# Conditioned residual product on one Trainium2 core: loads in 8 KB rows, zero blocks filled by ScalarE, placing shared with VectorE, first load in two parts

## What is computed

```python
w = weights[conditions]
return x + jnp.einsum('bct,bcd->bdt', x, w)
```

## Time and profile before

| | us |
|---|---|
| median of 3 runs | 48.3 |
| lowest, highest | 47.49, 48.56 |
| the profiled execution, its own time | 47.52 |
| its span in the profile | 45.6 |
| mean granted TensorE clock | 0.981 |

### The profile page before, as it was taken

One profiled execution on the slowest core, in us unless ns is written; L12 is line 12 of the kernel. 1 busy time (PEld: TensorE's weight loads), 2 busy tenths in 40 slices (PEclk: granted clock), 3 DMA queues, 4 the chain that ended last, 5 costly groups with the idle time before them and its releaser, 6 DMA issues.

```text
span 45.6 us, 301 instructions
## 1 busy us (share of the span) xinstructions
PE 23.4 (51%) x98; PEld 10.0 (22%) x98; DVE 14.9 (33%) x20; ACT 14.6 (32%) x18; POOL 2.6 (6%) x10
## 2 busy tenths in 40 slices
PE   0004000000000009999999789999999999930000
PEld 0004000000000004243527054534534434300000
DVE  0891000000003980009559290064064065550000
ACT  0820000000000009009999999062062063450000
POOL 4080900000000000000000000000000000000000
PEclk9999999999999999999999999999999999999975
DMA  0689999999999999999997999999998999999991
GB/s 0 108 338 431 424 417 431 417 439 424 431 431 511 431 403 417 388 460 460 460 331 280 403 424 453 381 489 446 460 417 338 431 446 403 424 439 388 417 406 47
DMA packets 2162, 17.83 MB, mean 391 GB/s; under 512 B 242, under 2 KB 242, under 8 KB 498
## 3 DMA queue, kind: packets, MB, share of 16 engines
q1 hardware_dynamic: 2016, 16.78, 89.1%
q0 software_dynamic: 144, 1.05, 5.4%
q10 hardware_dynamic: 2, 0.00, 0.0%
HBM read 9.44 MB, written 8.39 MB: 391 GB/s over the span
## 4 chain that ended last, share of the span: by engine, by line
PE 43%; DMA 21%; DVE 10%; ACT 7%; issue 5%; POOL 2%; POOLq 1%
PE product L156 31%; DMA gathered<-weights,table_row 21%; PE product L160 12%; DVE w_all L186 5%; ACT y_sb L116 4%; ACT w_diag L111 3%; POOL w_diag L128 2%; DVE w_diag L168 2%; DVE y_sb L195 2%; DVE gathered L183 1%; POOLq L36 1%; DVE piece L171 0%; DVE one L169 0%
## 5 line engine op out<-in xcount | busy, mean ns | idle before, releaser
L160 PE MATMUL product<-x_sb,w_all 64*64 64x512 f32 x64 | 8.9, 698 | 13.0 <-DVE w_all L186 12.9
L156 PE MATMUL product<-x_sb,w_diag 128*128 128x512 f32 x32 | 14.0, 594 | 0.3 <-issue 0.3
L191 DVE COPY y_sb<-product 128x1024 f32<-128x1024 f32 x7 | 8.6, 1225 | 12.6 <-PE product L156 7.2
L116 ACT COPY y_sb<-product 128x1024 f32<-128x1024 f32 x7 | 7.1, 1012 | 8.5 <-PE product L156 6.3
L111 ACT COPY w_diag<-w_all 64x256 f32<-64x256 f32 x8 | 5.1, 637 | 14.6 <-DVE w_all L186 14.4
L156 PEld LDWEIGHTS product<-x_sb,w_diag 128*128 128x128 f32 x32 | 6.0, 190 | 8.3 <-issue 8.3
L160 PEld LDWEIGHTS product<-x_sb,w_all 64*64 64x64 f32 x64 | 3.5, 207 | 17.6 <-DVE w_all L186 13.0
L183 DVE TENSOR_TENSOR gathered<-gathered,piece 128x64 f32<-128x64 f32 x1 | 0.3, 270 | 10.0 <-DMA gathered<-weights,table_row 10.0
L139 PE MATMUL product<-one,row_along 1*128 1x1 f32 x2 | 0.6, 344 | 3.6 <-DVE row_along L175 3.6
L186 DVE STREAM_TRANSPOSE w_all<-gathered 128x2048 f32<-128x2048 f32 x1 | 2.3, 2311 | 0.0
L195 DVE COPY y_sb<-product 128x512 f32<-128x512 f32 x2 | 1.4, 692 | 1.5 <-PE product L156 1.5
(11 more groups left out here) (4 smaller groups left out, 0.4 us busy)
## 6 DMA issues: line engine op xcount, KB each, us to landing
out<-y_sb SPq DMA_DIRECT2D x5, 1024.0 KB, 6.2
x_sb<-x SPq DMA_DIRECT2D x4, 1024.0 KB, 8.3
x_sb<-x SPq DMA_DIRECT2D x2, 2048.0 KB, 19.9
out<-y_sb SPq DMA_DIRECT2D x1, 2048.0 KB, 6.7
out<-y_sb SPq DMA_DIRECT2D x2, 512.0 KB, 4.3
condition<-conditions ACTq DMA_DIRECT2D x1, 0.2 KB
gathered<-weights,table_row POOLq DMA_INDIRECT x1, 9.7
```

The source lines that it names most:

```text
L116: nc.scalar.copy(y_sb[:, 4 * turn:4 * turn + 2, :], product[turn % SETS][0][:, :, :]).then_inc(moved_by_act, 1)
L156: product_of = nc.tensor.matmul(product[turn % SETS][j][:, g, :], w_diag[:, n - 4 * TILED, :], x_sb[:, n, :], start=True, stop=True)
L160: product_of = nc.tensor.matmul(product[turn % SETS][h][halves(g), j, :], w_all[halves(h), :, n], x_sb[halves(h), n, :], start=True, stop= ...
L191: nc.vector.tensor_copy(y_sb[:, 4 * turn + 2:4 * turn + 4, :], product[turn % SETS][1][:, :, :]).then_inc(moved_by_dve, 1)
```

## The change

Five edits are made together.

1. **8 KB rows.** `LOADS` and `STORES` are gone. Each turn is one load and one store of 1 MB (turn 7 is still stored in two halves), so nothing has 16 KB rows, and turn 2 is stored without waiting for turn 3.
2. **First load in two parts.** The load of turn 0 is issued as 16 partitions and then 112 partitions; TensorE waits for 32 on its semaphore. The other loads have semaphores of their own.
3. **Zeros by ScalarE.** The two memsets of `w_diag`'s off-diagonal blocks by VectorE and GpSimd are removed. VectorE sets a small tile `zero` (128x1), and ScalarE copies it, broadcast, to both blocks before it waits for `w_ready`.
4. **Shared placing.** ScalarE places only half 0 of each later turn, VectorE half 1, each ahead of its own move of the turn. TensorE waits for both.
5. VectorE's identity addition now waits for `pieces_set` itself, which GpSimd's removed memset no longer does.

```diff
-    LOADS = [(0, 0), (1, 1), (2, 2), (3, 3), (4, 5), (6, 7)]
-    STORES = [(0, 0), (1, 1), (2, 3), (4, 4), (5, 5), (6, 6)]
...
+        zero = sbuf("zero", [P, 1], fp32)
...
         def _(sp):
-            for first, last in LOADS:
-                pairs = pairs_of(first, last)
-                sp.dma_start(x_sb[:, pairs, :], x[:, pairs, :]).then_inc(x_loaded[first], 16)
-            for first, last in STORES:
-                sp.wait_ge(moved_by_act, last + 1)
-                sp.wait_ge(moved_by_dve, last + 1)
-                pairs = pairs_of(first, last)
-                sp.dma_start(out[:, pairs, :], y_sb[:, pairs, :]).then_inc(stored, 16)
+            for part in (slice(0, P // 8), slice(P // 8, P)):
+                sp.dma_start(x_sb[part, pairs_of(0), :], x[part, pairs_of(0), :]).then_inc(x_loaded[0], 16)
+            for turn in range(1, TURNS):
+                sp.dma_start(x_sb[:, pairs_of(turn), :], x[:, pairs_of(turn), :]).then_inc(x_loaded[turn], 16)
+            for turn in range(LAST):
+                sp.wait_ge(moved_by_act, turn + 1)
+                sp.wait_ge(moved_by_dve, turn + 1)
+                sp.dma_start(out[:, pairs_of(turn), :], y_sb[:, pairs_of(turn), :]).then_inc(stored, 16)
...
         def _(act):
             act.dma_start(condition[:, :, :], conditions).then_inc(condition_loaded, 16)
+            act.wait_ge(zero_set, 1)
+            for h in range(PAIR):
+                nc.scalar.copy(w_diag[halves(h), :, (1 - h) * D:(2 - h) * D],
+                               zero[halves(h), :].unsqueeze(2).to_broadcast([C, PAIRS - 4 * TILED, D])
+                               ).then_inc(w_zeroed, 1)
+            act.wait_ge(w_ready, 1)
             for turn in range(TURNS):
                 if turn < TILED:
-                    later = slice(4 * turn, 4 * turn + 4)
-                    act.wait_ge(w_ready, 1)
-                    for h in range(PAIR):
-                        nc.scalar.copy(w_diag[halves(h), later, h * D:(h + 1) * D],
-                                       w_all[halves(h), :, pairs_of(TILED + turn, TILED + turn)].rearrange("p d n -> p n d")
-                                       ).then_inc(w_placed, 1)
+                    nc.scalar.copy(w_diag[halves(0), pairs_of(turn), 0:D],
+                                   w_all[halves(0), :, pairs_of(TILED + turn)].rearrange("p d n -> p n d")
+                                   ).then_inc(w_placed_by_act, 1)
...
         def _(pool):
-            pool.wait_ge(pieces_set, 2 * (P // Q))
-            nc.gpsimd.memset(w_diag[halves(1), :, 0:D], 0.0).then_inc(w_zeroed, 1)
...
         def _(pe):
-                if turn in x_loaded:
-                    pe.wait_ge(x_loaded[turn], 16)
+                pe.wait_ge(x_loaded[turn], 32 if turn == 0 else 16)
...
                 if turn >= TILED:
-                    pe.wait_ge(w_placed, PAIR * (turn - TILED + 1))
+                    pe.wait_ge(w_placed_by_act, turn - TILED + 1)
+                    pe.wait_ge(w_placed_by_dve, turn - TILED + 1)
...
         def _(dve):
-            nc.vector.memset(w_diag[halves(0), :, D:PAIR * D], 0.0).then_inc(w_zeroed, 1)
+            nc.vector.memset(zero[:, :], 0.0).then_inc(zero_set, 1)
...
+            dve.wait_ge(pieces_set, 2 * (P // Q))
             dve.wait_ge(w_gathered, 16)
...
             for turn in range(LAST):
+                if turn < TILED:
+                    nc.vector.tensor_copy(w_diag[halves(1), pairs_of(turn), D:PAIR * D],
+                                          w_all[halves(1), :, pairs_of(TILED + turn)].rearrange("p d n -> p n d")
+                                          ).then_inc(w_placed_by_dve, 1)
                 dve.wait_ge(multiplied, turn + 1)
```

More of the change, by code:

```diff
@@ L58, in conditioned_residual_kernel @@
                    for s in range(SETS)]
-        x_loaded = {first: semaphore(f"x_loaded{first}") for first, _ in LOADS}
+        x_loaded = [semaphore(f"x_loaded{turn}") for turn in range(TURNS)]
         condition_loaded = semaphore("condition_loaded")
         one_set = semaphore("one_set")
+        zero_set = semaphore("zero_set")
         rows_along = semaphore("rows_along")
@@ L70, in conditioned_residual_kernel @@
         w_zeroed = semaphore("w_zeroed")
-        w_placed = semaphore("w_placed")
+        w_placed_by_act = semaphore("w_placed_by_act")
+        w_placed_by_dve = semaphore("w_placed_by_dve")
         multiplied = semaphore("multiplied")
@@ L79, in halves, with pairs_of @@
             return slice(h * C, (h + 1) * C)
-        def pairs_of(first, last):
-            return slice(4 * first, 4 * last + 4)
+        def pairs_of(turn):
+            return slice(4 * turn, 4 * turn + 4)
         def round_of(turn, j):
@@ L100, in _ @@
                 sp.dma_start(out[:, round_of(LAST, j), :], y_sb[:, round_of(LAST, j), :]).then_inc(stored, 16)
-            sp.wait_ge(stored, 16 * (len(STORES) + 2))
+            sp.wait_ge(stored, 16 * (TURNS + 1))
         @block.scalar
@@ L187, in _ @@
                                 ).then_inc(w_ready, 1)
+            dve.wait_ge(w_ready, 1)
             for turn in range(LAST):
+                if turn < TILED:
+                    nc.vector.tensor_copy(w_diag[halves(1), pairs_of(turn), D:PAIR * D],
+                                          w_all[halves(1), :, pairs_of(TILED + turn)].rearrange("p d n -> p n d")
+                                          ).then_inc(w_placed_by_dve, 1)
                 dve.wait_ge(multiplied, turn + 1)
```

## The result

The changed kernel takes 48.94 us (median of six executions, 48.52 to 49.39), the kernel before 47.88 us (six executions, 47.49 to 48.56). The ratio is 1.021, interval 1.011 to 1.031. So it is slower, and whether by more than 2% the interval leaves open; the forecast was 47.4 us with a range up to 48.5. The profiled execution took 49.24 us, span 47.5.

The account below looks back on a forecast made before the run. The full DMA queue was taken as the bound, with the engine chain beside it at zero slack. From the profiled 47.52 us, rows gave -0.1 and chain start, zeros, placing and first load 0: 47.4 us, range 46.8 to 48.5.

Parts of the forecast that it names:

- First load in two parts: First transfer of the load queue: bounds 0.4 us gained and 2.15 lost, taken as 0.
- The 16 partitions are slow: Rival, first transfer: 16 partitions load below full rate, costing up to 2.15 us; 48.4 us at 100 GB/s; chance 0.20.
- 8 KB rows: Turn from loads to stores: smaller rows recover part of the dip, 0.1 us gained, bounds 0.6 gained and 0.1 lost.
- For the queue of bytes all of this is worth 0: Start of the chain: issuing the gather earlier does not shorten the full DMA queue, 0 us; likewise for shared placing.
- Start of the chain: VectorE before the gather: shorter memsets start the row numbers 0 to 0.85 us earlier, 0.4 taken; gather lands equally earlier.
- GpSimd's memset ... its removal gives nothing: Start of the chain: the gather waits for VectorE's table_row, not GpSimd's memset, so removing that memset gains nothing.
- Shared placing: ScalarE and VectorE placing: every later store 0.8 us earlier, turn 6's store 1.2 with the gather, 0 for the queue.
- ScalarE's zeros: ScalarE before w_all: two copies end between 4.6 and 7.6 us, hidden by the wait for the gather, cost 0.
- The reading of two bounds side by side: Whole kernel: the queue of bytes and the engine chain up to turn 6's store both bound it, with about zero slack.
- The explanation of the spread by a late chain: Runs of 47.49 to 48.56 us: a chain late in some executions; 1.2 us of slack brings the median to 47.4.
- The change doesn't reach what makes the other runs slow: Rival, whole kernel: the spread comes from the transfers themselves, so chain slack buys nothing, median 48.2 us; chance 0.22.

Follow-up runs that it names:

- the split alone: The kernel before with only its first load split into 16 and 112 partitions: 48.84 us, ratio 1.007.
- whole loads without the hold: The changed kernel with its first load in one transfer of 128 partitions, first store not delayed: 48.43 us, ratio 1.010.
- halves: The changed kernel with its first load in two parts of 64 partitions each: 50.19 us, ratio 1.039.
- those of 16 KB and the faster engines: The changed kernel's zeros and placing with the transfers of the kernel before: 48.70 us, ratio 1.019.
- the pair of held kernels: First store waits for turn 6's load: kernel before with 8 KB rows 47.83 us (1.000), changed kernel with whole first load 47.39 us (0.990).

## Why the prediction was wrong, point by point

**The step that failed most is "First load in two parts", the value 0.** I took it by reasoning that the ramp is not held by a rate. The ramp did get better, by at most 0.75 x (284 - 197)/427 = 0.15 us, but it was not the place where the price stands. Early loss went from 0.5 to 1.5 us in the changed kernel and to 1.7 with the split alone: 1.0 to 1.2 us.

The rival *The 16 partitions are slow* had 0.20 and the number 48.4 at 100 GB/s; the executions without the late engine took 48.5 to 48.6. Its price came out at about that rate, and its place was wrong. The 16 partitions were carried at least as fast as the start of a whole load, and the 112 behind them were slow, which neither the forecast nor the rival had. That its sum comes out is luck in part too: it adds 1.0 to 47.4, and whole loads without the hold take 48.43, since they lose 1.1 us at the turn.

The page that spoke against the part (the Trainium skill, SBUF — State Buffer, "Door 1: The DMA port swizzle") gave 0.95 us and 48.3. The size agrees, but the trace doesn't bear out the reason for this split: the 0.95 us of the Trainium skill belong to the 16 partitions, whose packets were not slow. The port table there fits the halves better: by the Trainium skill partitions 0 to 63 reach 8 of 16 ports. Halves lost 2.4 us more than whole loads, near the 2.5 us by which a megabyte at half rate is longer.

**"8 KB rows", 0.1 gained,** had about the right size, by luck: the kernel before with rows of 8 KB took 47.5 us in two of its four executions, as the kernel before there at its best, and lost 0.3 us less at the turn. The row size was not what made the dip (0.2 us with rows of 8 KB, 1.3 us with those of 16 KB and the faster engines). The dip depends on how early the first store is queued.

**"For the queue of bytes all of this is worth 0"** failed for that reason. I took an earlier chain as free slack. With whole loads it costs 0.3 to 0.8 us more at the turn, because it queues the first store into the loads. In the changed kernel this does not show, as it has no turn loss; there the turn gave back 0.5 of what the split took. So the median of 47.4 needed two things, no loss from the split and none at the turn, and taking away the one brought the other. The kernel with the first load whole and the first store held has neither, and takes 47.39 us.

**"Start of the chain"**: the gather was issued 0.96 us earlier, outside the stated 0 to 0.85, and not for the stated reason: the row numbers started only 0.16 us earlier (2.20 against 2.36) and took 0.28 us and not 1.06. "GpSimd's memset ... its removal gives nothing" is probably the wrong sentence (see the last section). That the gather lands as much earlier, which I had assumed, failed beside the slowed loads: 0.27 us. **"Shared placing"**: VectorE's copies take 0.40 us (0.42 forecast), ScalarE's zeros 2.1 us as hidden as forecast. With the whole first load the large products started at 25.07 (25.2 forecast), in the changed kernel at 26.41. Of the 1.34 us between them 0.92 stand already at the first tiled product (15.84 against 16.76), behind the gather; the rest is the longer stretch of tiled products (9.30 against 9.72 us).

**The reading of two bounds side by side was right**, as the pair of held kernels shows. The explanation of the spread by a late chain was not. The kernel with the first load whole and the store held issues the store of turn 6 at 37.4, with slack, and its nine executions still lie at 47.16 to 48.58 us. Two things are seen in late executions. One is the instruction packet, which makes the span longer. The other lies outside the profile's rows: of 45 executions of the kernel before on the four chips 18 took over 48.3 us, and 11 of these had spans of 45.6 to 46.1, no longer than the others, with 2.5 to 3.0 us around the span and not about 1.9. Slack in the chain can't reach that. The rival *The change doesn't reach what makes the other runs slow* had this right, though it looked for the cause in the transfers; the cause is open.

The account of the changed kernel against the one before: +1.0 early loss, -0.5 at the turn, and +0.3 between 13 and 22 us (422 against 437 GB/s). That is 0.8 us, as in the spans (46.4 to 46.6 without the late engine, against 45.6 to 45.9). The remaining 0.2 to 0.3 us of the difference of the medians go with the executions with the late engine.

## What to carry to other kernels

When a DMA queue is full to the end, leave a transfer whole. Cut by partitions it ran at a lower rate here, in its second part too, the busy share doesn't show it, and no later stretch makes it good; cut along the free dimension it lost little rate, but that kernel was slower as well (1.028). Work out GB/s by windows and price each dip before asking which engine is late. And where loads and stores share a queue, issuing the first store as early as possible can cost more than it brings. A wait on the last load but one was worth 1.0 us with whole loads and the faster engine work, and nothing with the slower engine work or the split.

## What the runs showed of the hardware that was not expected

**VectorE's small operation ended only with GpSimd's memset.** In the kernel before L175 takes 1.06 us from 2.36 and ends at 3.42, just after GpSimd's memset (2.39 + 0.95). In the kernel with rows of 8 KB and the hold it started later and still ended at 3.42:

```profile
2.39 0.95 POOL L129 MEMSET w_diag<- 64x1024 f32 x1 [1.11 <-DVE piece L172]
2.55 0.87 DVE L176 TENSOR_SCALAR row_along<-condition 1x64 f32<-1x64 int32 x2 [0.22 <-DMA condition<-conditions]
```

Without that memset the same pair takes 0.28 us. The memset is no releaser of anything in the waits; if this is a wait, the profile shows it as VectorE's busy time. (The Trainium skill, SBUF — State Buffer, "SBUF: two separate sides", has a port pair that VectorE and GpSimd lock against each other; it names particular operations of VectorE, and whether this is one of them no row tells. The memset alone was not taken away in a run of its own.)

**The last load slows down when the first store is queued early behind it**, with whole loads to 307 GB/s over 4 us, and not when the store comes 2 us later. It did not with a load split by partitions early in the queue.

**A transfer to 112 partitions behind one to 16 is carried slower than one to all 128**: packets of 0.33 to 0.44 us and not 0.31 to 0.32, and the megabyte landed 1.1 us later.

**A 16 KB instruction packet can make one DMA engine over 1 us late**, at a time the kernel doesn't choose. It took 0.97 us in the changed kernel and stood in the profiles of five kernels while the queue was full (from 33.5 to 38.1 us), and each of these ended with a tail of one or a few engines. (The Trainium skill, Runtime: NRT & Kernel Launch, "Instruction fetch mechanics", says that instructions are fetched in blocks of 16 KiB and that the cost is mostly hidden. Here it was not: the landings of the stores behind the packet are spread by over 1 us.)
